# Score matmuls of a group in ascending order of block width

## The reference

```python
xn = layernorm(x)
q = (xn @ Wq).reshape(b, n, 16, 64)             # layer 1: q, k normalised per head
k, v = split(xn @ Wkv)                          # 64 channels each
k, v = concat(null_k, k), concat(null_v, v)     # 129 keys
sim = einsum('bhid,bjd->bhij', q, k) * scale + bias[h]
sim = where(causal or masked, -big, sim)        # row i sees the null key and keys 0..i
out = einsum('bhij,bjd->bhid', softmax(sim), v)
x = x + layernorm(out @ Wo)
```

## Time and profile before

| | |
|---|---|
| median of three runs | 2144.53 us (2143.86 to 2146.55) |
| profiled execution, its own time | 2146.16 us |
| its span, first to last instruction | 2144.4 us |
| PE / PEld busy | 2084.0 / 1860.3 us |
| DVE / ACT / POOL busy | 1601.1 / 1555.1 / 1027.0 us |
| score matmuls on L674 in the chain that ended last | 8% |

### The profile page before, as it was taken

The page is one execution under the profiler, slowest core; times in us unless marked ns, Lnnn a source line. Parts: engine busy times, 40 slices in busy tenths (PEclk is TensorE's granted clock), DMA queues, the critical chain, the costliest instruction groups (busy, mean ns, idle before and its releaser), DMA issues.

```text
span 2144.4 us, 72068 instructions
## 1 busy us (share of the span) xinstructions
PE 2084.0 (97%) x26363; PEld 1860.3 (87%) x26363; DVE 1601.1 (75%) x3422; ACT 1555.1 (73%) x6241; POOL 1027.0 (48%) x1510
## 2 busy tenths in 40 slices
PE   5899999999999999999999999999999999999987
PEld 4788988988988988988988988988988988988876
DVE  5877777777777777777777777777777777777765
ACT  3767777777777777777777777777777777777775
POOL 3445444445544444544544544544544544544543
PEclk8999999999999999999999999999999999999998
DMA  7212222222222212222222222222222212222211
GB/s 233 83 55 73 63 72 62 61 60 69 66 71 60 66 59 66 70 65 61 70 58 61 75 63 63 70 57 62 75 63 63 70 57 62 75 63 63 68 52 42
DMA packets 183034, 147.47 MB, mean 69 GB/s; under 512 B 121440, under 2 KB 125616, under 8 KB 182992
## 3 DMA queue, kind: packets, MB, share of 16 engines
q1 hardware_dynamic: 179008, 141.31, 22.3%
q10 hardware_dynamic: 3296, 4.46, 0.7%
q0 software_dynamic: 688, 1.14, 0.3%
HBM read 98.56 MB, written 37.77 MB: 64 GB/s over the span
## 4 chain that ended last, share of the span: by engine, by line
PE 92%; ACT 2%; SPq 2%; DVE 2%; issue 1%; POOL 1%; DMA 0%; POOLq 0%; DVEq 0%; ACTq 0%
PE psum L709 33%; PE psum L615 18%; PE psum L581 16%; PE psum L692 8%; PE psum L674 8%; PE psum L543 3%; PE psum L632 3%; PE psum L592 2%; SPq L386 1%; ACT o_hi L907 1%; ACT probs L901 1%; POOL probs L1479 0%; DMA xa<-in_x_dram 0%; DVE wo_lo L1188 0%; PE psum L623 0%
## 5 line engine op out<-in xcount | busy, mean ns | idle before, releaser
L901 ACT ACTIVATE probs<-probs,neg_max 128x129 f32<-128x129 f32 (+3 forms) x2048 | 712.3, 351 | 56.4 <-DVE neg_max L1144 56.3
L1469 POOL TENSOR_TENSOR masked_bias<-bias,pad_neg 128x516 f32<-128x516 f32 (+3 forms) x512 | 396.2, 806 | 211.8 <-DVE probs L1138 206.1
L1479 POOL TENSOR_TENSOR probs<-probs,den_inv 128x512 f32<-128x512 f32 (+3 forms) x512 | 369.4, 743 | 149.4 <-DVE den_inv L1149 149.4
L1491 POOL TENSOR_TENSOR y_out<-y_out,res 128x512 f32<-128x512 f32 x128 | 165.9, 1296 | 527.0 <-ACT y_out L865 527.0
L901 ACT ACTIVATION_READ_ACCUMULATOR probs<-probs,neg_max 128x1 f32 x2048 | 385.4, 188 | 0.0
L1154 DVE STREAM_TRANSPOSE probs_t<-probs 128x512 f32<-128x512 f32 (+3 forms) x512 | 229.9, 487 | 196.0 <-POOL probs L1479 194.9
L1138 DVE TENSOR_TENSOR probs<-psum,masked_bias 128x648 f32<-128x648 f32 x256 | 212.7, 831 | 114.3 <-PE psum L674 110.1
L709 PE MATMUL psum<-wo_hi,o_hi 128*128 128x512 f32 x1024 | 273.2, 409 | 8.2 <-ACT o_hi L907 7.5
L907 ACT ACTIVATE o_hi<-psum,null_v_col 128x512 fp32r<-128x512 f32 x256 | 162.1, 684 | 156.0 <-PE psum L692 156.0
L709 PE MATMUL psum<-wo_hi,o_lo 128*128 128x512 f32 x1024 | 262.5, 398 | 0.0
L709 PE MATMUL psum<-wo_lo,o_hi 128*128 128x512 f32 x1024 | 261.3, 397 | 0.0
(11 more groups left out here) (133 smaller groups left out, 3915.5 us busy)
## 6 DMA issues: line engine op xcount, KB each, us to landing
res<-in_x_dram SPq DMA_DIRECT2D x64, 256.0 KB, 2.7
v_rep<-v_kept SPq DMA_DIRECT2D x512, 32.0 KB, 1.8
x_of<-y_out SPq DMA_DIRECT2D x64, 256.0 KB, 2.1
res<-x_of SPq DMA_DIRECT2D x64, 256.0 KB, 2.7
out_dram<-y_out SPq DMA_DIRECT2D x64, 256.0 KB, 2.1
xa<-in_x_dram SPq DMA_DIRECT2D x63, 256.0 KB, 2.7
xa<-x_of SPq DMA_DIRECT2D x63, 256.0 KB, 2.7
q_aside<-qp SPq DMA_DIRECT2D x32, 256.0 KB, 3.1
```

Of the source, the lines that this page charges most:

```text
L901: x_ = nc.scalar.activation(s, s, ACT.Exp, bias=neg_max[:, b, n:n + 1], accum_out=den[:, b, n:n + 1])
L1469: m = nc.gpsimd.tensor_tensor(block(masked_bias, b), block(bias[u.layer], b), pad_neg[u.layer][:, 0:WIDTH[b]].unsqueeze(1).to_broadcast([P ...
L1479: m = nc.gpsimd.tensor_tensor(some, some, den_inv[:, b, :].unsqueeze(2).to_broadcast([P, 4, n]), ALU.mult)
```

## The change

The loop over the four blocks in `scores` runs upward instead of downward. It stands in every one of the 256 groups.

```diff
@@ -666,7 +666,7 @@
                 if not isinstance(u.done, int):
                     pe.sem_inc(pe_passed, 1)
                 tr = P if static(u, 0, 0) else TR
-                for b in (3, 2, 1, 0):
+                for b in range(BLOCKS):
                     for r in range(0, P, tr):
                         for e in range(2):
                             half = slice(e * DH, (e + 1) * DH)
```

## The result

Over nine runs each, the changed kernel takes 2152.29 us (2148.98 to 2154.05), and the kernel before 2146.55 (2143.86 to 2147.79; the three runs shown first lay at the low end of these). The ratio is 1.0026, with a 95% interval of 1.0017 to 1.0035: slower by 5.6 us, between 3.6 and 7.5. The forecast was 6.0 us more than before, or 2150.5 us against the median of the first three runs of before (2144.53); the measured time lies in its range of 2147.8 to 2153.5.

What follows compares the result with a forecast made beforehand. TensorE (PE) was taken to bound the kernel; 221 uncovered groups each losing 0.027 us to one more exposed load gave 6.0 us, so 2150.5 us against the median of 2144.53, range 2147.8 to 2153.5.

Steps and rivals of the forecast that it cites:

- PE as the bound, and a loss between phases as a loss of the kernel: Whole kernel: TensorE is busy 2084 of 2144.4 us and hardly waits, so a nanosecond lost between phases lengthens the kernel.
- One more exposed load, 0.027 us: Score groups: both 33-column quartets now have a load behind them, before only one; 0.75 us per group becomes 0.78.
- quartet: Score matmuls, L674: four 64x64 tiles starting within 0.02 us; eight per 64-row group, two each of 129, 97, 65, 33 columns.
- The record marks I gave: Profile after, from a group's first load: third quartet some 0.17 us, last 0.56, next load 0.78; last record to it 0.20.
- The end of a group costs 0.09 us after the stream, whatever the width: Where the tile shape changes, the next load waits for the last stream to end and 0.09 us more.
- 33 groups covered: Groups ahead of project_out (L709): the wait for ACT's o_hi leaves 0.25 us slack, so these 33 of 256 cost nothing.
- 221 x 0.027 = 6.0 us: Whole kernel: 221 groups, without the 33 covered and the first unit's two, each lose 0.027 us; 6.0 us in all.
- its 80%: Whole kernel: chance given to slower by over 0.2%, from 73 + 8 = 81% less 1 for a low median.
- Next load under the last stream: Group end, rival: next phase's weights load while the last 129-column quartet streams; -26 us, 2118 us; 3%.
- Cheap loads: Score groups, rival: loads take no longer than 33 columns stream, so groups shrink by 0.03; -6 us, 2138 us; 4%.
- Hidden elsewhere: Whole kernel, rival: more phases than the 33 are held by unnamed waits, under 4.3 us arrive; 2144.5 to 2148.5 us; 12%.
- Instruction supply inside a group: Group's front, rival: the sequencer can't deliver three narrow quartets fast enough, up to 0.03 us more per group; 2157 us; 8%.

Runs made afterwards that it cites:

- e6: Against the kernel before: blocks ascending only in group 0, the one computed a stage ahead (128 groups); 2150.17 us, ratio 1.0019.
- e10: Against the kernel before: the 33-column block computed twice in one group of a loop pass, group 1 of stage first; 2150.03 us, ratio 1.002.
- e11: Against the kernel before: the 33-column block computed twice in both groups of stage first; 2153.62 us against 2145.45, one run.
- e2: Against the kernel before: blocks in the order 65, 97, 129, 33 columns, ascending but the narrowest last; 2146.05 us, ratio 0.9999.
- e4: Against the kernel before: the 33-column block computed twice in all groups, the second time at the end; 2338.03 us, ratio 1.0903.
- e1: Against the kernel before: blocks in the order 33, 129, 97, 65 columns; 2152.8 us, ratio 1.0033.
- e13: Against the kernel before: blocks in the order 33, 65, 129, 97 columns; 2151.01 us against 2146.23, one run.
- e3: Against the kernel before: ascending only in the group ahead of project_out in stages second and second0 (31 groups); 2145.59 us, ratio 0.9995.
- e8: The changed kernel measured once more, against the kernel before; 2151.2 us, ratio 1.003.
- e12: Against the kernel before: blocks in the order 65, 33, 97, 129 columns; 2152.44 us against 2146.23, one run.
- e9: Against the kernel before: the 33-column block computed twice in group 0 only, four groups a pass; 2346.7 us, ratio 1.0944.

## Why the prediction was right

- **PE as the bound, and a loss between phases as a loss of the kernel.** Right. PE's share and waits are as before, and e6, e10 and e11 show added nanoseconds in a group arriving in the pass one for one.
- **One more exposed load, 0.027 us.** Right: 28 ns per group (752 to 781). The term that carries it, a quartet taking the longer of its stream and its successor's load, is shown from both sides, by e2 (33 last: nothing) and e4 (58 ns for each added one). One of its supports was misread: L725's matmuls are not about 0.10 us apart but 0.112, and half of that, 0.056, fits the 0.055 better. The record marks I gave: last quartet at 0.56, next load at 0.78, last record to next load 0.20, all came. The third quartet's record I put at 0.17; it is at 0.14, since it too starts ahead of its weights, the very reading that I had used for the eighth quartet of before and forgot here.
- **The end of a group costs 0.09 us after the stream, whatever the width.** Right for 33, 65, 97 and 129 columns: from the last record to the next phase's load it is 148, 147, 172 and 198 ns (before, e1, e13, the change), of which the scaled stream is 28, 54, 81 and 108 and, in the first, 30 the wait for weights. The Trainium skill, "TensorEngine Tiling (Array Packing)", Key Properties, says that a change of tiling mode drains the engine. The trace agrees, with these 0.09 us and no load ahead of them. That it is the change of tile and not the end of a phase, the prediction took for granted; the trace of before shows it where L615 hands over to L709 and the tile stays 128x128. PE's last matmul there, and then the load behind it:

```profile
1006.97 0.34 PE L615 MATMUL psum<-w_hi,x_lo 128*128 128x384 f32 x1
```

```profile
1006.98 0.36 PEld L709 LDWEIGHTS psum<-wo_lo,o_hi 128*128 128x128 f32 x2
```

  The next phase's load starts 3 ns after the last matmul, under its stream, and its first matmul at 1007.15, with no gap.
- **33 groups covered.** Right, shown by e3 for the 31 that it reorders.
- **221 x 0.027 = 6.0 us.** That the measured 5.6 came so close is in part luck: two terms were off in opposite directions, and the interval is wide. The groups make 7 x 0.028 x 29 = 5.7 us in the loop, and outside it 18 open ones 0.5 and the first unit's two 0.05 and 0.16, 6.4 in all. The prediction put the change of all other phases at nothing and gave no reason; that failed: they gave back 0.07 us a pass, 2.0 us in 29 passes (1.5 in e8). By the pass the change should be 4.4 to 4.9 us slower, the runs say 5.6 (3.6 to 7.5) and 6.4 (3.9 to 9.0). That 4.4 lies just at the 0.2% from which I called it slower; the forecast of the sign had less margin than its 80% suggests.
- **The rivals.** Next load under the last stream: fell. Between the last quartet's loads (from 1029.60) and 1029.92 none starts, and in 217 of the 219 full groups ahead of L692 or L543 in the changed kernel's trace the next load comes 198 or 199 ns after the last 129-column record. Cheap loads: fell by e4. Hidden elsewhere: fell as a wait, but its size was partly there in the shorter phases. Instruction supply inside a group: not seen in e2 nor in the change, where the three narrow quartets keep the load's pace, and behind the loop's jump, where the group was 29 ns longer already before, it grows by the same 28.

**Open:** what shortens the other phases. It is not the group's length (e1's groups are 27 ns longer, like the change's, and give 3 ns back), and not the program alone (the change and e8, and e12 within one execution). It goes with a group 1 that ends in 97 or 129 columns, but e12 shows that such an ending is not enough. Why it should matter is not shown. I take it for a matter of how PE's starts fall against something that ticks at another rate, but that is a guess: no run shows what, and none tried to shift PE by a few ns and nothing else.

## What to carry to other kernels

In a row of independent matmuls on tiles like these (64x64, FP32, a load of 0.055 to 0.058 us), each one costs the longer of its own stream and the load behind it. So put one whose stream is shorter than a load at the end, if a change of tile follows: there the next load waits anyway. Where the tile stays the same, the next phase's load comes under the stream, and the last place should win nothing; no run here tried that. Price a reordering by the starts of load records in one group, then count which groups end in a wait that covers the difference. For effects of 0.1 to 0.3%, measure the repeat distance of the loop in the trace as well as the run times, and look at every pass, since a mean can hide two patterns (e12).

## What was not expected of the hardware

- A loop whose pass holds 1705 to 1737 PE records runs with 26 instruction packets in all; with 1769 records it fetches some 250 more and stands 4.1 us at each jump back (3.6 with 1833), after which the clock is granted at 1.2 GHz for some 6 us. Beyond what the added quartets cost by themselves that is 5.8 us a pass in e4 and 6.7 in e9. The kernel before sits only 32 to 64 records below that edge. The number of records sorts these kernels; whether code size is what counts, no run shows by itself.
- Work that was not touched changed its length by up to 8 ns in 3.7 us, in steady patterns, by 20 ns a pass between two executions of one program (e8), and by 54 ns between passes of one execution (e12). In a kernel that is 97% bound by one engine that is a third of the effect studied.
